# Graph convolution passes: ScalarE makes three of four classes of one-hot rows, and TensorE looks up one more column per block

## The chip, the cores and the metric

One core of a Trainium2 chip runs the whole program. The metric is the device time of one execution in microseconds. The median of three runs of the kernel before is 13509.75 us (13502.95 to 13512.86).

## The reference, cut to what matters

Four graph layers run one after the other on 6250 nodes and 200000 edges that are sorted by destination, each followed by a layer norm. The change touches the third layer alone, which holds three graph convolutions:

```python
def gcn_conv(x, w, b, row, col, ew, n):
    h = x @ w
    deg = jax.ops.segment_sum(ew, col, num_segments=n)
    dinv = jnp.where(deg > 0, jax.lax.rsqrt(deg), 0.0)
    norm = dinv[row] * ew * dinv[col]
    out = jax.ops.segment_sum(norm[:, None] * h[row], col, num_segments=n)
    return out + b
...
x2 = jax.nn.relu(gcn_conv(x, w1, b1, row, col, ew, n))
x3 = jax.nn.relu(gcn_conv(x2, w2, b2, row, col, ew, n))
x4 = jax.nn.relu(gcn_conv(x3, w3, b3, row, col, ew, n))
```

For each edge a row of a node table is looked up by the edge's source, scaled by the edge's weight, and summed over the edges of one destination.

## The kernel before, in words

`graph_pass` does one such convolution. It is called three times: twice with rows of 16 numbers (the narrow passes) and once with rows of 32 (the wide pass). The edges lie as 128 partitions by 1568 columns. A block is 16 columns; a pass has 98 blocks, which alternate between two halves `h` = 0 and 1 with their own buffers. A loop of 49 rounds handles block n = 2i and then n = 2i + 1.

A column's 128 rows are looked up in one of two ways.

- GpSimd gathers them from DRAM by an indirect DMA (L990), one instruction per column. In a narrow pass that is 7 columns for half 0 and 8 for half 1; in the wide pass 10.
- TensorE looks up the others: `ON_CHIP` gives 9 and 8 columns in a narrow pass and 6 and 6 in the wide one. The node table lies on the chip in four classes of 13 nodes per lane. For each class a 0/1 matrix `one_lo` says which lane an edge's source has; a column takes 4 classes times 2 parts of the table, so 8 matmuls (L1030). `multiply(h, 0)` does the first four columns (three in the wide pass), `multiply(h, 1)` the rest. VectorE then picks one of the 13 nodes per lane (`pick`, a product L1078, and `gather`, a reduction L1081).

`one_lo` is made on VectorE by `one_hots` (L1048): four compares per block, one per class, of the keys with the lane's number. The keys of a block come by a DMA from SyncE's queue (L960) that spreads one row of DRAM to 128 partitions.

The order within a pass is written out by hand, engine by engine, with semaphores between. VectorE in block n: `pick(0)`, the compares for block n+1, the small `one_slots` for n+1, `gather(0)`, `pick(1)`, `gather(1)`, then, after the gathered rows have landed, the scaling (L1106), a carry (L1109) and a scan along the block (L1113). ScalarE in block n: after the gathered rows have landed it copies the index of block n+2 (L996), after the scan it copies the result into `run_rows` (L1018), and then it stages four small tiles for block n+2. SyncE in block n: it waits until the compares have read the keys of block n, loads the keys of block n+2 (L960), waits for the `copied` semaphore of block n (which `run_rows` raises), and stores `run_rows` (L975). TensorE is about a block ahead of VectorE: its first multiply of block n+1 waits for the step ONE_HOTS of VectorE's block n, its second for SECOND_MADE, which is `pick(1)`. The semaphore `looked` counts the multiplies that are done.

Of the kernel before, what the change touches and what calls it, by code (L numbers as in the profile page):

```python
# [22 lines left out]
ACT = mybir.ActivationFunctionType  # L23
AX = mybir.AxisListType

P = 128
# [8 lines left out]
IT = T // (2 * B)  # L35
# [10 lines left out]
SENT = 1 + C + LABELS  # L46
RUN = C + LABELS + 2 * C
GROUP_SLOTS = 7
ON_CHIP = {16: (9, 8), 32: (6, 6)}
FIRST_GROUP = {16: 4, 32: 3}  # L50
CLASSES = 4
CLASS = -(-J // CLASSES)
KEY_BLOCKS = -(-T // P)
WIDE_CLASSES = 7
# [851 lines left out]
def graph_pass(nc, sig, table, width, edge, parts, running, final, zeros):  # L906
# [6 lines left out]
    GATHERED = [B - K for K in KS]  # L913
    GROUPS = [[slice(0, FIRST), slice(FIRST, K)] for K in KS]
    MOST = [FIRST, max(KS) - FIRST]
    FIRST_MADE, ONE_HOTS, SECOND_MADE, SCALED, per = 1, 1 + CLASSES, CLASSES + 4, CLASSES + 6, CLASSES + 8
    INIT = 2 * per
    SLOT = 256 if CLASS * width <= 256 else 512
    with ExitStack() as ctx:
# [8 lines left out]
        def sem(name):  # L928
            return ctx.enter_context(nc.semaphore(f"{name}{uid}"))
# [21 lines left out]
            weight = [t[:] for t in pair("weight", [P, B])]  # L951
        gathered, stored, indexed, staged, loaded = ([sem(f"{n}{h}_") for h in range(2)] for n in ("gathered", "stored", "indexed", "staged", "loaded"))
        stepped, looked, copied = (sem(n) for n in ("stepped", "looked", "copied"))
        block = ctx.enter_context(nc.Block())
        running_v = running[0:EP, :].rearrange("(p t) c -> p t c", p=P)

        @block.sync
        def _(sp):
            def load(h, n):
                sp.dma_start(keys[h][:], edge["keys"][bass.ds(n * B, KS[h]), :].rearrange("k e -> (k e)").unsqueeze(0).broadcast_to([P, KS[h] * P])).then_inc(loaded[h], 16)  # L960

            for h in range(2):
                cut = slice(h * width // 2, (h + 1) * width // 2)
                sp.dma_start(running[EP:EP + 1, cut], zeros[0:1, cut]).then_inc(stored[h], 16)
            for h in range(2):
                load(h, h)
            with sp.Fori(0, IT) as i:
                for h in range(2):
                    n = 2 * i + h

                    sp.wait_ge(stepped, INIT + per * (n - 1) + ONE_HOTS)
                    load(h, n + 2)

                    sp.wait_ge(copied, n + 3)
                    sp.dma_start(running_v[:, bass.ds(n * B, B), :], run_rows[h][:]).then_inc(stored[h], 16)  # L975
            for h in range(2):
                sp.wait_ge(stored[h], 16 * (IT + 1))
                sp.wait_ge(loaded[h], 16 * (IT + 1))
# [14 lines left out]
        @block.scalar  # L993
        def _(act):
            def stage_index(h, at):
                nc.scalar.copy(index[h][:], edge["src"][:, bass.ds(at + KS[h], GATHERED[h])]).then_inc(indexed[h], 1)  # L996

            def stage(h, at):
                nc.scalar.activation(slot[h][:], edge["src_slot"][:, bass.ds(at, KS[h])], ACT.Copy)
                nc.scalar.activation(weight[h], edge["weight"][:, bass.ds(at, B)], ACT.Copy)  # L1000
                nc.scalar.activation(keep[h][:], edge["keep"][:, bass.ds(at, B)], ACT.Copy)
                nc.scalar.activation(carried[h][:, :, 1:B], repeat(edge["keep"][:, bass.ds(at + 1, B - 1)], width), ACT.Copy).then_inc(staged[h], 1)

            act.sem_inc(copied, 2)
            stage_index(0, 0)
            stage_index(1, B)
            stage(0, 0)
            stage(1, B)
            with act.Fori(0, IT) as i:
                for h in range(2):  # L1010
                    n = 2 * i + h

                    act.wait_ge(gathered[h], 16 * GATHERED[h] * (i + 1))
                    stage_index(h, (n + 2) * B)

                    act.wait_ge(stepped, INIT + per * (n + 1))
                    act.wait_ge(stored[h], 16 * (i + 1))
                    nc.scalar.activation(run_rows[h][:], run[h][:].rearrange("p c b -> p b c"), ACT.Copy).then_inc(copied, 1)  # L1018
                    stage(h, (n + 2) * B)

        @block.tensor
        def _(pe):
            def multiply(h, g):
                for k in range(KS[h] - FIRST if g else FIRST):
                    at = k * SLOT
                    to = p_slots[g][:, at // 512, at % 512:at % 512 + width * CLASS]
                    e = (g * FIRST + k) * P
                    for q in range(CLASSES):
                        for part_no, part in enumerate(parts):
                            ins = nc.tensor.matmul(to, one_lo[h][:, q, e:e + P], flat(part[:, q, :, :]),  # L1030
                                                   start=q == 0 and part_no == 0, stop=q == CLASSES - 1 and part_no == len(parts) - 1)
                ins.then_inc(looked, 1)

            with pe.Fori(0, IT) as i:
                for h in range(2):
                    n = 2 * i + h

                    pe.wait_ge(stepped, INIT + per * (n - 1) + ONE_HOTS)
                    multiply(h, 0)

                    pe.wait_ge(stepped, INIT + per * (n - 1) + SECOND_MADE)
                    multiply(h, 1)

        @block.vector
        def _(dve):
            def one_hots(h, step):
                for q in range(CLASSES):
                    step(nc.vector.tensor_scalar(one_lo[h][:, q, :], keys[h][:], sig["lanes"][:, q:q + 1], None, ALU.is_equal))  # L1048

            def one_slots(h, step):  # L1050
                step(nc.vector.tensor_tensor(one_hi[h][:], repeat(sig["iota"][:, 0:CLASS], KS[h]), spread(slot[h][:], CLASS), ALU.is_equal))
# [7 lines left out]
            dve.wait_ge(loaded[0], 16)  # L1059
            one_hots(0, lambda ins: ins.then_inc(stepped, 1))  # L1060
            dve.wait_ge(staged[0], 1)
            one_slots(0, lambda ins: ins.then_inc(stepped, per - FIRST_MADE - CLASSES))
            with dve.Fori(0, IT) as i:
                for h in range(2):
                    n, done = 2 * i + h, [0]
# [14 lines left out]
                    def gather(g):  # L1080
                        step(nc.vector.tensor_reduce(rows[h][:, GROUPS[h][g], :], picked[g][:, 0:KS[h] - FIRST if g else FIRST, :, :], AX.X, ALU.add))  # L1081

                    dve.wait_ge(looked, 2 * n + 1)

                    after()
                    pick(0)
# [3 lines left out]
                    one_hots(1 - h, step)  # L1090
                    assert done[0] == ONE_HOTS

                    dve.wait_ge(staged[1 - h], i + 1 + h)
                    one_slots(1 - h, step)
                    after(FIRST_MADE)
                    gather(0)

                    dve.wait_ge(looked, 2 * n + 2)
                    pick(1)
                    assert done[0] == SECOND_MADE  # L1100
                    after()
# [13 lines left out]

            dve.wait_ge(stepped, INIT + per * 2 * IT)
            nc.vector.tensor_copy(final[:, 0:width], run[1][:, :, B - 1]).then_inc(stepped, 1)


def spread_to_edges(nc, sig, block, node_rows, begin_row, edge_rows, table, first_key, first_rows, saved=0):  # L1120
# [903 lines left out]
def gnn(nc, out, x, src, dst, u, ew, labels, label_rows, attrs, spline1, root1, bias01, spline2, root2, bias02,  # L2024
# [3 lines left out]
    with ExitStack() as ctx:  # L2028
# [3 lines left out]
        def sb(name, shape, dt=F32, scope=ctx):  # L2032
            return scope.enter_context(nc.sbuf_tensor(name, shape, dt))

        sig = {n: Signal(ctx.enter_context(nc.semaphore(n))) for n in
               ("copied", "turned", "turned_sb", "product", "saved", "fetched", "pe_step", "act_step", "dve_step", "pool_step", "moved", "rounds")}


        groups = [Signal(ctx.enter_context(nc.semaphore(f"fetched_group{g}"))) for g in range(J // GROUP_SLOTS)]
# [28 lines left out]
        for name in ("ident", "ones", "upper", "shift1", "shift2"):  # L2068
            sig[name] = sb(name, [P, P])
        sig["iota"], sig["lanes"] = sb("iota", [P, P]), sb("lanes", [P, WIDE_CLASSES])  # L2070
        sig["ident_b"], sig["not_earlier"] = sb("ident_b", [P, P], BF16), sb("not_earlier", [P, P], BF16)
        chunk_row = sb("chunk_row", [P, 1])
        zeros = sb("zeros", [P, max(B, J - REST) * C])
# [155 lines left out]
        with ExitStack() as tmp:  # L2229
            h = sb("h0", [P, J, C], F32, tmp)  # L2230
            with ExitStack() as made:
                wide_key, in_class = (sb(n, [P, T], F32, made) for n in ("wide_key", "in_class"))
                rest = sb("x_rest", [P, J, C], F32, made)

                def wide_keys(step):

                    step(V.tensor_scalar(in_class[:], src_hi[:, 0:T], -float(WIDE_CLASS // 2), 1.0 / WIDE_CLASS, ALU.add, ALU.mult))
                    step(V.tensor_scalar(in_class[:], in_class[:], ROUND, None, ALU.add))
                    step(V.tensor_scalar(in_class[:], in_class[:], -ROUND, None, ALU.add))
                    step(V.scalar_tensor_tensor(wide_slot[:, 0:T], in_class[:], -float(WIDE_CLASS), src_hi[:, 0:T], ALU.mult, ALU.add))  # L2240
                    step(V.scalar_tensor_tensor(wide_key[:], in_class[:], float(P), src_lo[:, 0:T], ALU.mult, ALU.add))

                with nc.Block() as block:
                    on_vector(nc, sig, wide_keys, block)
                    turn_keys(nc, sig, block, made, wide_key, wide_key_rows)
                    on_vector(nc, sig, lambda step: split_wide(nc, xs[:], rest, x_parts, step), block)
                    carry_masks(nc, sig, first_dst_f[:], last_dst_f[:], link, step_pen, use_pen, block, made)
# [400 lines left out]
```

## Time and profile before

| what | value |
|---|---|
| median of the runs | 13509.75 us |
| span of the profiled execution | 13509.6 us |
| VectorE busy | 11066.4 us (82%) |
| TensorE matmuls busy | 9536.4 us (71%) |
| GpSimd busy | 9266.9 us (69%) |
| ScalarE busy | 4374.5 us (32%) |
| first keys of the first narrow pass and of the wide pass are issued at | 8250.1 and 10388.5 us |

The shares are over all four layers; the three passes lie between 8250 us and 11660 us of the span. What bounds a pass is read from the rows of that pass, not from the shares. GpSimd's instruction of a gather prepares the DMA's descriptors; between two of them lie 0.30 us that the profile calls issue.

### The profile page before, as it was taken

How to read it: one execution, taken by the hardware profiler on the slowest of the kernel's cores; microseconds unless marked ns; L12 is line 12 of the kernel's file. 1: busy time of each engine (PE TensorE's matmuls, PEld its weight loads, DVE VectorE, ACT ScalarE, POOL GpSimd, SP SyncE). 2: the span in 40 equal slices, each digit the busy share in tenths (PEclk: the TensorE clock that was granted, in tenths of full speed). 3: DMA queues.
4: the chain of work that ended last, by engine and by line, in shares of the span. 5: the costliest groups of instructions: out<-in, count | busy, mean ns of one | idle time of the engine just before them, and what ended most of it. 6: DMA issues, size and time to landing. Idle time of an engine off the chain costs nothing. (4 is left out here: it accounts for less than half of the span.)

```text
span 13509.6 us, 209667 instructions
## 1 busy us (share of the span) xinstructions
PE 9536.4 (71%) x57073; PEld 8046.3 (60%) x57073; DVE 11066.4 (82%) x24500; ACT 4374.5 (32%) x14847; POOL 9266.9 (69%) x9348
## 2 busy tenths in 40 slices
PE   5666667777757766777774546886886888678886
PEld 4555556666645555555552116886886777567775
DVE  8888878888768888888888997886886888589997
ACT  3444434444423333333333331111111111123332
POOL 6777757777667777777774005777776777677776
PEclk8888879999878888888886667998997999699997
DMA  3333324444323333333335761221221222133332
GB/s 89 89 89 85 88 71 125 124 119 124 113 65 100 99 101 101 101 100 97 99 101 195 272 246 41 48 47 39 47 48 38 50 49 49 30 78 87 85 87 68
DMA packets 637171, 1243.59 MB, mean 92 GB/s; under 512 B 206033, under 2 KB 390390, under 8 KB 586530
## 3 DMA queue, kind: packets, MB, share of 16 engines
q1 hardware_dynamic: 322624, 912.21, 19.9%
q0 software_dynamic: 300160, 269.02, 11.8%
q10 hardware_dynamic: 14337, 61.82, 1.2%
q8 instruction: 16, 0.26, 0.0%
q14 instruction: 34, 0.28, 0.0%
HBM read 475.84 MB, written 768.08 MB: 92 GB/s over the span
## 5 line engine op out<-in xcount | busy, mean ns | idle before, releaser
L1030 PE MATMUL p_slots<-part,one_lo 128*128 128x208 f32 (+1 forms) x18032 | 2666.9, 312 | 616.3 <-DVE one_lo L1048 615.9
L990 POOL DMA_INDIRECT rows<-gcn_table,index x2450 | 2442.6, 997 | 883.0 <-issue 727.7
L1030 PEld LDWEIGHTS p_slots<-part,one_lo 128*128 128x128 f32 x18032 | 2584.2, 205 | 699.2 <-DVE one_lo L1048 682.7
L1351 PE MATMUL a_p_slots<-att_part,a_one_lo 128*128 128x456 f32 x8232 | 2007.5, 408 | 585.2 <-DVE y L1414 502.8
L1351 PEld LDWEIGHTS a_p_slots<-att_part,a_one_lo 128*128 128x128 f32 x8232 | 1741.4, 214 | 953.6 <-DVE y L1414 680.7
L1282 POOL DMA_INDIRECT sent<-a_out_rows,a_place x1568 | 1585.5, 1011 | 494.0 <-issue 476.2
L622 PE MATMUL p_slots<-x_part,key_lo 128*128 128x448 f32 x6916 | 1649.2, 393 | 109.7 <-DVE scratch L751 73.3
L556 POOL DMA_INDIRECT msg<-x_rows,index x1372 | 1312.0, 956 | 507.4 <-issue 448.4
L556 POOL DMA_INDIRECT msg<-h_rows,index x1274 | 1234.4, 969 | 490.9 <-issue 383.8
L622 PEld LDWEIGHTS p_slots<-x_part,key_lo 128*128 128x128 f32 x6916 | 1378.1, 206 | 226.3 <-DVE scratch L751 90.3
L788 DVE SCALAR_TENSOR_TENSOR run<-run,keep,msg 128x129 f32<-128x129 f32 (+1 forms) x3136 | 1112.8, 355 | 388.7 <-ACT msg L591 284.2
L1744 POOL DMA_INDIRECT e_rows<-soft_table,e_index x1176 | 1167.4, 993 | 375.6 <-issue 330.8
L1787 PE MATMUL e_p_slots<-soft_part,e_one_lo 128*128 128x456 f32 x5488 | 1243.9, 387 | 125.2 <-DVE e_one_lo L1810 125.2
L1787 PEld LDWEIGHTS e_p_slots<-soft_part,e_one_lo 128*128 128x128 f32 x5488 | 1073.9, 198 | 260.3 <-DVE e_one_lo L1810 146.4
L1273 POOL DMA_INDIRECT a_rows<-att_table,a_index x980 | 998.9, 1019 | 305.7 <-issue 298.4
L1048 DVE TENSOR_SCALAR one_lo<-keys,lanes 128x1152 fp32r<-128x1152 f16 (+2 forms) x1188 | 826.4, 756 | 10.6 <-DMA keys<-key_rows 10.6
L996 ACT COPY index<-src_i 128x8 int32 (+4 forms) x300 | 59.2, 198 | 2286.4 <-DMA rows<-gcn_table,index 2176.6
L591 ACT ACTIVATE msg<-msg,weight 128x64 f32<-128x64 f32 x3136 | 769.1, 340 | 0.5 <-DVE msg L769 0.5
L584 ACT ACTIVATE earlier<-p_same 128x1280 bf16<-128x1280 f32 x392 | 485.2, 1238 | 787.8 <-PE p_same L637 787.8
L1078 DVE TENSOR_TENSOR picked<-p_slots,one_hi 128x832 f32<-128x832 f32 (+1 forms) x588 | 704.1, 1198 | 37.3 <-PE p_slots L1030 27.2
L1081 DVE TENSOR_REDUCE rows<-picked 128x64 f32<-128x832 f32 (+1 forms) x588 | 702.3, 1194 | 10.1
L1367 PE MATMUL a_p_label<-w_labels,a_label 128*128 128x512 f32 x392 | 340.8, 1021 | 467.4 <-DMA a_label_row<-in_label_rows 467.4
(478 smaller groups left out, 17203.7 us busy)
## 6 DMA issues: line engine op xcount, KB each, us to landing
running_dst<-a_run SPq DMA_DIRECT2D x98, 1600.0 KB
running_src<-s_run SPq DMA_DIRECT2D x98, 1600.0 KB
running<-run SPq DMA_DIRECT2D x98, 1032.0 KB
running<-run SPq DMA_DIRECT2D x98, 1024.0 KB
running<-y SPq DMA_DIRECT2D x98, 656.0 KB
s_rows<-sent ACTq DMA_DIRECT2D x98, 584.0 KB, 7.0
begun_x<-zeros SPq DMA_DIRECT2D x98, 512.0 KB
a_xdst<-begun_x SPq DMA_DIRECT2D x98, 512.0 KB
```

The source lines that it names most:

```text
L556: pool.indirect_dma_start(out=msg[h][:, K + k, 0:C], out_offset=None, in_=table, in_offset=offsets(index[h][:, k:k + 1])).then_inc(gathere ...
L591: nc.scalar.activation(msg[h][:, k, C:2 * C], msg[h][:, k, 0:C], ACT.Copy, scale=weight[h][:, k:k + 1]).then_inc(weighed, 1)
L622: ins = nc.tensor.matmul(p_slots[:, bank, 0:C * WIDE_CLASS], key_lo[h][:, c, e:e + P], flat(part[:, c, :, :]), start=c == 0 and part_no == ...
L788: step(nc.vector.scalar_tensor_tensor(run[h][:, k, :], before, keep[h][:, k:k + 1], msg[h][:, k, :], ALU.mult, ALU.add))
L990: pool.indirect_dma_start(out=rows[h][:, KS[h] + k, :], out_offset=None, in_=table, in_offset=offsets(index[h][:, k:k + 1])).then_inc(gath ...
L1030: ins = nc.tensor.matmul(to, one_lo[h][:, q, e:e + P], flat(part[:, q, :, :]), start=q == 0 and part_no == 0, stop=q == CLASSES - 1 and pa ...
L1048: step(nc.vector.tensor_scalar(one_lo[h][:, q, :], keys[h][:], sig["lanes"][:, q:q + 1], None, ALU.is_equal))
L1273: pool.indirect_dma_start(out=rows[h][:, K + k, :], out_offset=None, in_=table, in_offset=offsets(index[h][:, k:k + 1])).then_inc(gathered ...
L1282: pool.indirect_dma_start(out=sent, out_offset=offsets(place[h][:, k:k + 1]), in_=out_rows[h][:, k, :], in_offset=None).then_inc(scattered ...
L1351: ins = nc.tensor.matmul(to[:, k, 0:WIDE_COLUMNS], one_lo[h][:, q, e:e + P], part[:, q, :], start=q == 0 and part_no == 0, stop=q == WIDE_ ...
L1744: pool.indirect_dma_start(out=rows[h][:, KS[h] + k, :], out_offset=None, in_=table, in_offset=offsets(index[h][:, k:k + 1])).then_inc(gath ...
L1787: ins = nc.tensor.matmul(p_slots[g][:, k, 0:WIDE_COLUMNS], one_lo[h][:, q, e:e + P], part[:, q, :], start=q == 0 and part_no == 0, stop=q ...
```

## The change

Four things change in `graph_pass`; outside it one small constant is added (`lane_bias` = -2 times the lanes' numbers).

1. TensorE looks up one column more per block: 10 and 9 in a narrow pass, 7 and 7 in the wide one. GpSimd gathers one less: 6 and 7, and 9.
2. VectorE makes one of the four classes (`OWN` = 1). ScalarE makes the other three in `light`: three Squares of 2 key - 2 lane, which give 0 on a hit and at least 4 elsewhere, and one Relu of 1 minus that over all three classes in place, which gives 1 and 0. `light` for block n+2 stands at the head of ScalarE's block n, ahead of the index copy, and waits for the keys of block n+2 and for both multiplies of block n, whose `one_lo` it overwrites.
3. TensorE's first multiply of a block waits for `lit`, which ScalarE raises after the Relu. SyncE waits for `lit` of block n before it loads the keys of block n+2.
4. VectorE's `gather(0)` stands ahead of `one_slots`.

```diff
-ON_CHIP = {16: (9, 8), 32: (6, 6)}
+ON_CHIP = {16: (10, 9), 32: (7, 7)}
...
+LIT = 3
...
                     sp.wait_ge(stepped, INIT + per * (n - 1) + ONE_HOTS)
+                    sp.sem_inc(sig["rounds"].sem, 1)
+                    sp.wait_ge(lit.sem, lit.base + n + 1)
                     load(h, n + 2)
 
                     sp.wait_ge(copied, n + 3)
...
+            def light(h, n, loads):
+
+                act.wait_ge(loaded[h], 16 * loads)
+                for q in range(OWN, CLASSES):
+                    ins = nc.scalar.activation(one_lo[h][:, q, :], keys[h][:], ACT.Square, bias=sig["lane_bias"][:, q:q + 1], scale=2.0)
+                ins.then_inc(squared.sem, 1)
+                act.wait_ge(squared.sem, squared.base + n + 1)
+                nc.scalar.activation(one_lo[h][:, OWN:CLASSES, :], one_lo[h][:, OWN:CLASSES, :], ACT.Relu, bias=sig["ones"][:, 0:1], scale=-1.0).then_inc(lit.sem, 1)
...
             with act.Fori(0, IT) as i:
                 for h in range(2):
                     n = 2 * i + h
+
+                    act.wait_ge(looked, 2 * n + 4)
+                    light(h, n + 2, i + 2)
 
                     act.wait_ge(gathered[h], 16 * GATHERED[h] * (i + 1))
                     stage_index(h, (n + 2) * B)
...
                     pe.wait_ge(stepped, INIT + per * (n - 1) + ONE_HOTS)
+                    pe.wait_ge(lit.sem, lit.base + n + 1)
                     multiply(h, 0)
...
             def one_hots(h, step):
-                for q in range(CLASSES):
+                for q in range(OWN):
...
+                    after(FIRST_MADE)
+                    gather(0)
+
                     dve.wait_ge(staged[1 - h], i + 1 + h)
                     one_slots(1 - h, step)
-                    after(FIRST_MADE)
-                    gather(0)
...
```

SyncE's queue in the loop of the first narrow pass, before (an ISA or REGISTER_ALU row is one of the sequencer's own; the names in brackets are the semaphores it waits for):

```order
L960 ISA [waits stepped6771]
L960 DMA keys_6771<-key_rows 128x1152
L974 REGISTER_ALU
L975 ISA [waits copied6771]
L975 DMA running<-run_rows_6771 128x256
L971 ISA
L960 ISA [waits stepped6771]
L960 DMA keys_6771<-key_rows 128x1024
```

and of the change:

```order
L976 REGISTER_ALU [waits stepped6773]
L963 ISA [waits lit]
L963 DMA keys_6773<-key_rows 128x1280
L979 REGISTER_ALU
L980 ISA [waits copied6773]
L980 DMA running<-run_rows_6773 128x256
L974 ISA
L963 ISA [waits stepped6773,lit]
L963 DMA keys_6773<-key_rows 128x1152
```

The order on this queue is as it was: load of keys, wait for the copied result, store, load of the next keys. A wait for `lit` is added ahead of each load.

ScalarE's queue in the same loop, half 0, before:

```order
L996 ISA [waits gathered0_6771]
L996 COPY index_6771<-src_i 128x7
L1016 ISA
L1017 REGISTER_ALU [waits stepped6771]
L1018 ACTIVATE run_rows_6771<-run_6771 128x256 [waits stored0_6771]
L999 ISA
L999 ACTIVATE slot_6771<-src_hi 128x9
```

and of the change:

```order
L1011 ISA [waits looked6773]
L1013 ACTIVATE one_lo_6773<-keys_6773,lane_bias 128x1280 [waits loaded0_6773]
L1013 ACTIVATE one_lo_6773<-keys_6773,lane_bias 128x1280 x2
L1015 REGISTER_ALU
L1016 ACTIVATE one_lo_6773<-one_lo_6773,ones 128x3840 [waits squared]
L1032 ISA
L1001 ISA [waits gathered0_6773]
L1001 COPY index_6773<-src_i 128x6
L1035 ISA
L1036 REGISTER_ALU [waits stepped6773]
L1037 ACTIVATE run_rows_6773<-run_6773 128x256 [waits stored0_6773]
```

The three Squares and the Relu now stand between one block's staging and its index copy and `run_rows`, behind two waits: for TensorE and for the keys.

## Rows read from the trace of the kernel before

**Rows 1.** Stretches of the first narrow and the wide pass; columns named in the first line
```profile
core 0: us, PE busy (x) PEld busy (x) DVE busy (x) ACT busy (x) POOL busy (x), PEclk, DMA share, GB/s
8270.00:9210.00 940.00, 806.08 (x6498) 790.07 (x6496) 806.71 (x1144) 139.84 (x575) 721.74 (x709) 0.93 0.23 48
...
10410.00:11630.00 1220.00, 992.62 (x4631) 943.09 (x4629) 1017.71 (x1162) 204.60 (x581) 926.62 (x963) 0.91 0.23 49
```

**Rows 2.** The scan L1113, once per block: count, ns min/median/max, first and last start
```profile
L1113 DVE TENSOR_TENSOR_SCAN run<-carried,p_msg x90: 686/686/689, 8271.0 to 9148.9; 128x256 f32<-128x256 f32 x90
...
L1113 DVE TENSOR_TENSOR_SCAN run<-carried,p_msg x98: 1220/1220/1222, 10410.1 to 11634.8; 128x512 f32<-128x512 f32 x98
```

**Rows 3.** Groups of the first narrow pass, then of the wide: busy us, mean ns | idle before
```profile
L990 POOL DMA_INDIRECT rows<-gcn_table,index x709 | 722.4, 1019 | 218.4 <-issue 215.5 <-DVE p_msg L1109 1.8 <-DVE p_msg L1106 0.9
L1078 DVE TENSOR_TENSOR picked<-p_slots,one_hi 128x832 f32<-128x832 f32 x144 | 146.9, 1020 | 5.6 <-PE p_slots L1030 2.3
...
L1048 DVE TENSOR_SCALAR one_lo<-keys,lanes 128x1152 fp32r<-128x1152 f16 x192 | 144.7, 815 | 0.0
...
L990 POOL DMA_INDIRECT rows<-gcn_table,index x963 | 928.0, 964 | 293.7 <-issue 276.6 <-DVE p_msg L1109 17.1
```

**Rows 4.** Timeline of two narrow blocks: start us, us, engine line op [idle before]
```profile
8603.02 0.67 ACT L1018 ACTIVATE run_rows<-run 128x256 f32<-128x256 f32 x1 [1.40 <-DVE run L1113]
...
8603.80 3.04 DVE L1048 TENSOR_SCALAR one_lo<-keys,lanes 128x1152 fp32r<-128x1152 f16 x4
...
8604.51 0.34 SPq L960 DMA_DIRECT2D keys<-key_rows  x1
8605.11 1.12 POOL L990 DMA_INDIRECT rows<-gcn_table,index  x1 [0.30 <-issue]
...
8606.90 8.29 PE L1030 MATMUL p_slots<-part,one_lo 128*128 128x208 f32 x72 [1.70 <-DVE one_lo L1048]
...
8607.97 0.94 POOL L990 DMA_INDIRECT rows<-gcn_table,index  x1 [0.30 <-issue]
...
8613.11 0.66 ACT L1018 ACTIVATE run_rows<-run 128x256 f32<-128x256 f32 x1 [1.25 <-DVE run L1113]
...
8614.87 0.34 SPq L960 DMA_DIRECT2D keys<-key_rows  x1
```

**Rows 5.** Timeline of two wide blocks
```profile
10709.51 1.08 ACT L1018 ACTIVATE run_rows<-run 128x512 f32<-128x512 f32 x1 [2.17 <-DVE run L1113]
...
10711.42 0.34 SPq L960 DMA_DIRECT2D keys<-key_rows  x1
...
10713.48 11.54 PE L1030 MATMUL p_slots<-part,one_lo 128*128 128x416 f32 x48 [3.93 <-DVE one_lo L1048]
...
10721.80 1.12 ACT L1018 ACTIVATE run_rows<-run 128x512 f32<-128x512 f32 x1 [2.08 <-DVE run L1113]
...
10724.01 0.34 SPq L960 DMA_DIRECT2D keys<-key_rows  x1
...
10725.72 9.35 PE L1030 MATMUL p_slots<-part,one_lo 128*128 128x416 f32 x48 [0.70 <-DVE one_lo L1048]
```

**Rows 6.** First load of keys of a narrow pass and the compare that waits for it
```profile
8250.11 7.04 SPq L960 DMA_DIRECT2D keys<-key_rows  x3
...
8253.61 3.01 DVE L1048 TENSOR_SCALAR one_lo<-keys,lanes 128x1152 fp32r<-128x1152 f16 x4 [3.63 <-DMA keys<-key_rows]
```

**Rows 7.** The keys' DMAs of the wide pass, from issue to landing
```profile
DMA to landing us min/median/max: 3.1/3.4/4.0
```

**Rows 8.** ScalarE by shape over the whole program: busy us, mean ns | idle before
```profile
L1312 ACT ACTIVATE a_out_rows<-a_xdst,a_att 128x64 f32<-128x64 f32 x1568 | 385.1, 334 | 3.2
...
L1776 ACT ACTIVATE y<-e_run 128x1296 f32<-128x1296 f32 x98 | 247.0, 2521 | 370.5 <-DVE e_run L1905 370.5
...
L1002 ACT ACTIVATE carried<-keep 128x240 f32 x196 | 76.7, 391 | 0.0
...
L1002 ACT ACTIVATE carried<-keep 128x480 f32 x98 | 58.1, 592 | 0.0
```

More of the change, by code:

```diff
@@ L915, in graph_pass @@
     MOST = [FIRST, max(KS) - FIRST]
-    FIRST_MADE, ONE_HOTS, SECOND_MADE, SCALED, per = 1, 1 + CLASSES, CLASSES + 4, CLASSES + 6, CLASSES + 8
+    OWN = CLASSES - LIT
+    FIRST_MADE, ONE_HOTS, SECOND_MADE, SCALED, per = 1, 1 + OWN, OWN + 4, OWN + 6, OWN + 8
     INIT = 2 * per
@@ L953, in graph_pass @@
         stepped, looked, copied = (sem(n) for n in ("stepped", "looked", "copied"))
+        squared, lit = sig["squared"], sig["lit"]
         block = ctx.enter_context(nc.Block())
@@ L1008, in _ @@
             stage(1, B)
+            light(0, 0, 1)
+            light(1, 1, 1)
             with act.Fori(0, IT) as i:
@@ L1032, in multiply @@
                 ins.then_inc(looked, 1)
+            pe.sem_inc(looked, 2)
             with pe.Fori(0, IT) as i:
@@ L1061, in _ @@
             dve.wait_ge(staged[0], 1)
-            one_slots(0, lambda ins: ins.then_inc(stepped, per - FIRST_MADE - CLASSES))
+            one_slots(0, lambda ins: ins.then_inc(stepped, per - FIRST_MADE - OWN))
             with dve.Fori(0, IT) as i:
@@ L1081, in gather @@
                         step(nc.vector.tensor_reduce(rows[h][:, GROUPS[h][g], :], picked[g][:, 0:KS[h] - FIRST if g else FIRST, :, :], AX.X, ALU.add))
-                    dve.wait_ge(looked, 2 * n + 1)
+                    dve.wait_ge(looked, 2 * n + 3)
                     after()
@@ L1091, in _ @@
                     assert done[0] == ONE_HOTS
+                    after(FIRST_MADE)
+                    gather(0)
                     dve.wait_ge(staged[1 - h], i + 1 + h)
                     one_slots(1 - h, step)
-                    after(FIRST_MADE)
-                    gather(0)
-                    dve.wait_ge(looked, 2 * n + 2)
+                    dve.wait_ge(looked, 2 * n + 4)
                     pick(1)
@@ L1117, in _ @@
             nc.vector.tensor_copy(final[:, 0:width], run[1][:, :, B - 1]).then_inc(stepped, 1)
+        squared.base += 2 * IT + 2
+        lit.base += 2 * IT + 2
 def spread_to_edges(nc, sig, block, node_rows, begin_row, edge_rows, table, first_key, first_rows, saved=0):
@@ L2035, in gnn @@
         sig = {n: Signal(ctx.enter_context(nc.semaphore(n))) for n in
-               ("copied", "turned", "turned_sb", "product", "saved", "fetched", "pe_step", "act_step", "dve_step", "pool_step", "moved", "rounds")}
+               ("copied", "turned", "turned_sb", "product", "saved", "fetched", "pe_step", "act_step", "dve_step", "pool_step", "moved", "rounds", "squared", "lit")}
         groups = [Signal(ctx.enter_context(nc.semaphore(f"fetched_group{g}"))) for g in range(J // GROUP_SLOTS)]
@@ L2070, in gnn @@
         sig["iota"], sig["lanes"] = sb("iota", [P, P]), sb("lanes", [P, WIDE_CLASSES])
+        sig["lane_bias"] = sb("lane_bias", [P, WIDE_CLASSES])
         sig["ident_b"], sig["not_earlier"] = sb("ident_b", [P, P], BF16), sb("not_earlier", [P, P], BF16)
@@ L2235, in wide_keys @@
                 def wide_keys(step):
+                    step(V.tensor_scalar(sig["lane_bias"][:], sig["lanes"][:], -2.0, None, ALU.mult))
                     step(V.tensor_scalar(in_class[:], src_hi[:, 0:T], -float(WIDE_CLASS // 2), 1.0 / WIDE_CLASS, ALU.add, ALU.mult))
```

## The prediction

> **What bounds the kernel now.** I read the stretches of the passes first, because the page's shares run over four layers. In the first narrow pass VectorE is busy 807 of 940 us, TensorE 806, GpSimd 722 [rows 1]: three engines near their limit. The scan, one per block, gives the period: 89 intervals from 8271.0 to 9148.9 us are 9.86 us a block, and 97 intervals of the wide pass 12.63 [rows 2]. Then the groups. A narrow gather takes 1.019 us and 218.4 us of idle time lie between 709 of them, 0.31 each; 1.33 times 7.5 gathers is 9.9 us, the whole period [rows 3]. Wide, 0.964 + 0.305 is 1.27, times 10 is 12.7 [rows 3]. So GpSimd's issue of gathers bounds all three passes, and nearly all of its idle time is its own issue, not a wait. ScalarE has room: 139.84 us of 940, or 1.5 us of each of 95.3 blocks [rows 1].
>
> **What the change takes away.** One gather of 7.5 goes in a narrow pass: GpSimd's floor becomes 6.5 x 1.33 = 8.6 us. Wide, 9 x 1.27 = 11.4. VectorE's 807 / 95.3 = 8.5 us lose three compares of up to 0.815 (2.4) and gain one column in a product and a reduction, about 2 x 1.02 / 4 = 0.5 [rows 3]: 6.6 us, no bound any more. TensorE does 72 matmuls in 8.29 us in a narrow block [rows 4], 0.115 each; the mean of 76 takes 8.75. Wide it did 48 in 9.35 [rows 5], so 56 take 10.9. If nothing else held, all passes would gain.
>
> In the timeline a gather beside the compares took 1.12 us, one after them 0.94 [rows 4]; the wide mean is 0.964 [rows 3]. The Trainium skill, SBUF — State Buffer, section "Who interferes with whom", says that a VectorE operation in a two-port mode (a tensor_scalar may be one) locks GpSimd out of a port pair that it needs. By that rule the removed compares would bring a wide gather to some 0.95, and 9 x 1.25 = 11.25 instead of 11.4, 15 us less over the pass. I leave the sum at 11.4.
>
> **What it adds to ScalarE.** No row shows Square or Relu, so I price them by other ACTIVATEs. 240 columns take 391 ns and 480 take 592 [rows 8]: 0.84 ns a column. A 64-column one with a per-partition operand takes 334 [rows 8], so 0.28 us stand beside the columns (0.19 without such an operand); both new operations have one as bias. Square of 1280 columns: 1.35 us; of 1152: 1.25; of 896: 1.03. Relu of 3840: 3.50; 3456: 3.17; 2688: 2.53. Consecutive ones overlap by some 0.1 by my estimate, between none and 0.15, and the Relu waits for the last Square (0.1, estimated). `light` then takes 2 x 1.25 + 1.35 + 0.1 + 3.50 = 7.45 for ten columns and 6.8 for nine, 7.1 on the mean; wide 5.55. The lower bound, without the operand's cost, is 6.7. The upper bound is the row of 1296 columns in 2521 ns [rows 8], 1.73 ns a column, or 13.5 us; that one reads a permuted tile and ours are contiguous, so I take the near row.
>
> With its other 1.5 us ScalarE would be busy 8.6 us a narrow block. That alone would still fit into 9.86.
>
> The Trainium skill, ScalarE: Activation LUTs, section "Rules for kernel authors", advises VectorE rather than ScalarE for such simple functions. The rows agree as to price: three compares cost VectorE about 2.4 us, their replacement 7.1. By the rule alone the move loses only if ScalarE ends on the path.
>
> **Why it does end on the path.** The keys decide. SyncE's queue is in order: load keys(n+2), wait for `run_rows`(n), store, load keys(n+3). Before, VectorE wanted keys(n+3) only in its block n+2, more than a block later. Now ScalarE wants keys(n+3) at the head of its block n+1, right behind the staging of block n, while SyncE may load them only after ScalarE's `run_rows`(n). That closes a ring of one block:
>
> - `run_rows`(n) starts to keys(n+3) issued: 8603.02 to 8604.51 and 8613.11 to 8614.87 [rows 4], 1.49 and 1.76, mean 1.63. The added `lit` wait is long fulfilled; for its step I add 0.05 (0 to 0.1).
> - issue to landing: 3.4, from 3.1 to 4.0, for the wide keys of 128 x 768 two-byte numbers [rows 7]; the 128 x 1152 at a narrow pass's start took 8250.11 to 8253.61, so 3.5 [rows 6]. I take 3.5 for 1280 and 1152 columns, and 0.05 to wake.
> - `light`(n+3): 7.1.
> - index copy and start of `run_rows`(n+1), whose scan and gathers are done: 0.05.
>
> The sum is 12.4 us a narrow block, against 9.86. While the keys come, ScalarE stages for about a microsecond and then idles; that wait is new. Behind it on ScalarE stand the Squares, the index copy that GpSimd waits for two blocks ahead, and `run_rows`; TensorE's first multiply waits for the Relu. No other chain needs as much: TensorE 8.75, GpSimd 8.6, VectorE 6.6.
>
> The wide ring: 1.91 and 2.21 [rows 5], mean 2.06, + 0.05 + 3.4 + 0.05 + 5.55 + 0.05 = 11.15. That lies just below GpSimd's 11.4 and above TensorE's 10.9. With three chains so close I take 11.5, between 11.25 and, with no gain, 12.6.
>
> Start of a pass: before, the first narrow scan came 21 us after the first keys' issue [rows 2, 6]. Now `light`(0) stands ahead of the first multiply, and `light`(2) waits for both multiplies of block 0: 7.45 + 7.45 in place of four compares (3.0) and some cover, so about 10 us more per pass, 30 in all (15 to 40). The extra constant and the moved `gather(0)` cost nothing: VectorE has 5 us to spare per block.
>
> The sum: 2 x 98 x (12.4 - 9.86) = +498; 98 x (11.5 - 12.63) = -111; +30. The profiled span is 13509.6 and the median 13509.75, so no correction is due: 13,927, said as 13,925 us.
>
> **Rivals.**
>
> - *The key load is hidden* (faster). If keys land before ScalarE asks, the narrow passes run at TensorE's 8.75, say 9.0 with hand-overs, and the wide at 11.4: 196 x -0.86 - 98 x 1.23 + 20 = -270, 13,240 us. For it: every engine's own work is under the old period. Against: SyncE's order has the load behind `run_rows` in both programs, and `run_rows` now stands behind `light`. Chance 0.09.
> - *TensorE loses its clock and becomes the bound* (slower still). It would idle 3.6 us of each narrow block. The wide pass before had such a gap: after 3.93 us idle, 48 matmuls took 11.54 instead of 9.35 [rows 5], yet the granted clock was 0.91 of 2.4 GHz over the pass [rows 1]. At 1.2 GHz throughout, 76 matmuls would need 17.5 us; halfway, the narrow block is 14.5 and the time 13,925 + 196 x 2.1 = 14,335. Against: one such dip adds 2 to 3 us, 8.75 + 3 is still under 12.4, and the keys' landing gives slack of several us. Chance 0.05. The Trainium skill, TensorE: Matmul & The Clock Gate, section "What's actually happening", has the half clock as the idle default, released by activity; by that rule alone this rival would be likelier, and the trace's 0.91 bears it out only in part.
> - *ScalarE at the permuted row's rate*: `light` of 13.5 us, wide 10.2, periods 18.8 and 15.8: 13,510 + 1,752 + 311 + 30 = 15,600. Chance 0.03.
>
> The forecast keeps 0.83. With each piece at its low end (1.49, 3.1, 6.7, no steps) the narrow ring is 11.4 to 11.6, at the high end (1.86, 4.0, 7.5, 0.2) 13.5. With the wide from 11.25 to 12.6 that gives 13,700 to 14,250; I take 13,690 to 14,130 for eight in ten, which leaves the fast rival and most of the slow ones out. A difference under 0.2% (27 us) can't be told from none: slower 0.88, same 0.03, faster 0.09.
>
> **What would show it.** In the changed trace: narrow scans 12 to 13 us apart; before each first Square an idle stretch of 3 to 4 us that ends with the DMA of the keys; a Relu of 3840 columns near 3.5 us; keys issued 1.5 to 1.9 us after each `run_rows` starts; TensorE waiting for `one_lo` of ScalarE; GpSimd waiting for the index. The prediction is wrong if the Squares start without a wait for keys, if they end up waiting for TensorE, or if the narrow period is under 10 us.

## Result and profile after

The changed kernel takes 13904.47 us (median of four runs, 13892.0 to 13932.39) against 13506.35 for the kernel before: the ratio is 1.0294, 95% interval 1.0281 to 1.0307. It is slower by 398 us, as forecast (13,925). On the chip of a later series it took 13892.41 us and the ratio was 1.0280 (1.0263 to 1.0297).

The profiled execution spans 13901.5 us, 391.9 more than before. Two stretches, in the first narrow pass and in the wide one, with the columns of [rows 1]:

```profile
8400.00:9400.00 1000.00, 810.99 (x6239) 799.22 (x6239) 574.05 (x740) 680.84 (x822) 526.33 (x535) 0.88 0.18 41
11000.00:12000.00 1000.00, 953.75 (x4933) 915.68 (x4932) 841.34 (x794) 651.51 (x884) 759.23 (x791) 1.00 0.24 57
```

In the narrow pass VectorE fell from 86% to 57% and GpSimd from 77% to 53%; TensorE, at 81% after 86%, hardly changed, and ScalarE rose from 15% to 68%. No engine is busy throughout. An engine that is busy 68% of the time and still sets the end is part of a ring with waits in it. The scans of the three passes, as in [rows 2]:

```profile
L1135 DVE TENSOR_TENSOR_SCAN run<-carried,p_msg x98: 686/686/690, 8315.9 to 9493.7; 128x256 f32<-128x256 f32 x98
...
L1135 DVE TENSOR_TENSOR_SCAN run<-carried,p_msg x98: 686/686/690, 9612.3 to 10807.1; 128x256 f32<-128x256 f32 x98
...
L1135 DVE TENSOR_TENSOR_SCAN run<-carried,p_msg x98: 1220/1220/1222, 10929.9 to 12028.4; 128x512 f32<-128x512 f32 x98
```

Over 97 intervals that is 12.14, 12.32 and 11.32 us a block, where it was 9.87, 9.87 and 12.63. The waits of the narrow stretch (engine line, awaited: us in total, times, longest):

```profile
DVE one_hi L1072 <- ACT carried L1007: 374.5, 82, 5.4
POOL rows L995 <- ACT index L1001: 332.8, 82, 4.7
ACT one_lo L1013 <- DMA keys<-key_rows: 316.5, 82, 4.2
PEld p_slots L1049 <- ACT one_lo L1016: 200.6, 66, 4.7
```

VectorE, GpSimd and TensorE all wait for ScalarE, and ScalarE waits once in each of 82 blocks for the keys, 3.9 us each. One turn of the ring, in the timeline:

```profile
8601.24 0.64 ACT L1037 ACTIVATE run_rows<-run 128x256 f32<-128x256 f32 x1
...
8603.12 0.34 SPq L963 DMA_DIRECT2D keys<-key_rows  x1
...
8606.54 3.87 ACT L1013 ACTIVATE one_lo<-keys,lane_bias 128x1280 fp32r<-128x1280 f16 x3 [4.05 <-DMA keys<-key_rows]
...
8610.44 3.50 ACT L1016 ACTIVATE one_lo<-one_lo,ones 128x3840 fp32r<-128x3840 f32 x1
8613.84 0.18 ACT L1001 COPY index<-src_i 128x6 int32 x1
8613.93 0.64 ACT L1037 ACTIVATE run_rows<-run 128x256 f32<-128x256 f32 x1
8613.99 11.53 PE L1049 MATMUL p_slots<-part,one_lo 128*128 128x208 f32 x80 [4.39 <-ACT one_lo L1016]
...
8614.91 0.94 POOL L995 DMA_INDIRECT rows<-gcn_table,index  x1 [3.87 <-ACT index L1001]
```

`run_rows` to the issue of the keys 1.88 us, issue to the first Square 3.42, Squares and Relu 7.40, and `run_rows` follows at once: 12.7 us for a block of ten columns. TensorE starts 0.05 us after the Relu ends, GpSimd soon after the index copy.

The groups of the same two stretches, as in [rows 3, 8]:

```profile
L995 POOL DMA_INDIRECT rows<-gcn_table,index x535 | 527.3, 986 | 474.0 <-ACT index L1001 332.8 <-issue 141.1
L1013 ACT ACTIVATE one_lo<-keys,lane_bias 128x1280 fp32r<-128x1280 f16 x123 | 158.8, 1355 | 163.1 <-DMA keys<-key_rows 163.1
...
L1016 ACT ACTIVATE one_lo<-one_lo,ones 128x3840 fp32r<-128x3840 f32 x41 | 143.3, 3494 | 1.3
...
L995 POOL DMA_INDIRECT rows<-gcn_table,index x791 | 760.7, 962 | 241.1 <-issue 226.7 <-ACT index L1001 6.1 <-DVE run L1135 5.8
L1013 ACT ACTIVATE one_lo<-keys,lane_bias 128x896 fp32r<-128x896 f16 x264 | 256.2, 1034 | 335.4 <-DMA keys<-key_rows 335.4
L1016 ACT ACTIVATE one_lo<-one_lo,ones 128x2688 fp32r<-128x2688 f32 x88 | 223.9, 2544 | 2.9
```

Narrow, 333 of GpSimd's 474 idle us are waits for the index. Wide, its idle time is its own issue, as before; 9 x (0.962 + 0.305) is 11.4 us, within 1% of the period of 11.32.

### The profile page after: what moved, and what is told of

Its sections match the earlier page's. It is cut to its first block and busy times, and to the rows that moved or that the text cites. A ratio compares the mean times of both kernels' runs of the same rounds, so it can differ in the third digit from the quotient of the medians.

```text
span 13901.5 us, 216105 instructions
## 1 busy us (share of the span) xinstructions
PE 9885.1 (71%) x59425; PEld 8398.8 (60%) x59425; DVE 10674.4 (77%) x23610; ACT 6268.1 (45%) x16047; POOL 8921.5 (64%) x9054
## 3 DMA queue, kind: packets, MB, share of 16 engines
q0 software_dynamic: 290752, 265.79, 10.7%
## 5 line engine op out<-in xcount | busy, mean ns | idle before, releaser
L1049 PE MATMUL p_slots<-part,one_lo 128*128 128x208 f32 (+1 forms) x20384 | 2991.2, 311 | 635.9 <-ACT one_lo L1016 599.2
L1049 PEld LDWEIGHTS p_slots<-part,one_lo 128*128 128x128 f32 x20384 | 2921.7, 206 | 705.6 <-ACT one_lo L1016 640.7
L995 POOL DMA_INDIRECT rows<-gcn_table,index x2156 | 2105.2, 976 | 1553.4 <-ACT index L1001 821.9
L1013 ACT ACTIVATE one_lo<-keys,lane_bias 128x1280 fp32r<-128x1280 f16 (+2 forms) x900 | 1033.7, 1212 | 1159.9 <-DMA keys<-key_rows 1143.1
L1016 ACT ACTIVATE one_lo<-one_lo,ones 128x3840 fp32r<-128x3840 f32 (+2 forms) x300 | 922.1, 3074 | 9.8
L1099 DVE TENSOR_TENSOR picked<-p_slots,one_hi 128x832 f32<-128x832 f32 (+1 forms) x588 | 791.1, 1345 | 134.5 <-PE p_slots L1049 127.6
L1072 DVE TENSOR_TENSOR one_hi<-iota,slot 128x130 f32<-128x130 f32 (+2 forms) x297 | 81.5, 275 | 946.8 <-ACT carried L1007 946.8
L1102 DVE TENSOR_REDUCE rows<-picked 128x64 f32<-128x832 f32 (+1 forms) x588 | 787.2, 1339 | 10.2
```

Source lines behind the costliest of these rows:

```text
L995: pool.indirect_dma_start(out=rows[h][:, KS[h] + k, :], out_offset=None, in_=table, in_offset=offsets(index[h][:, k:k + 1])).then_inc(gath ...
L1013: ins = nc.scalar.activation(one_lo[h][:, q, :], keys[h][:], ACT.Square, bias=sig["lane_bias"][:, q:q + 1], scale=2.0)
L1016: nc.scalar.activation(one_lo[h][:, OWN:CLASSES, :], one_lo[h][:, OWN:CLASSES, :], ACT.Relu, bias=sig["ones"][:, 0:1], scale=-1.0).then_in ...
```

## Experiments

Theory A is the ring of the prediction. Theory B is that ScalarE's work bounds the narrow pass wherever the keys land. Theory C is that TensorE with one more column does.

**Keys ahead.** SyncE loads keys(n+3) before it waits for `run_rows`(n).

```diff
+            sp.wait_ge(stepped, INIT - per + ONE_HOTS)
+            sp.wait_ge(lit.sem, lit.base + 1)
+            load(0, 2)
...
-                    sp.wait_ge(stepped, INIT + per * (n - 1) + ONE_HOTS)
+                    sp.wait_ge(stepped, INIT + per * n + ONE_HOTS)
                     sp.sem_inc(sig["rounds"].sem, 1)
-                    sp.wait_ge(lit.sem, lit.base + n + 1)
-                    load(h, n + 2)
+                    sp.wait_ge(lit.sem, lit.base + n + 2)
+                    load(1 - h, n + 3)
...
```

> The changed kernel with one difference: SyncE loads the keys of block n+3 ahead of its wait for run_rows of block n, no longer behind the store. Theory A (the ring run_rows, load of keys, landing, light, next run_rows sets the narrow period): the 1.7 us to the issue and the 3.5 us to landing leave the ring; ScalarE's own 8.6 us and TensorE's 8.75 us remain, so narrow blocks of about 9.1 us (8.8 to 9.6), wide still 11.3 by GpSimd; time 13,300 us (13,220 to 13,420), faster than both kernels. Theory B (ScalarE's work and its hand-overs bound it, wherever keys land): narrow stays near 12.2, time within 50 us of 13,904. Theory C (TensorE with one more column and a falling clock is the bound): also 12.2 and 13,904.

13156.02 us; 0.9755 of before (0.9739 to 0.9771). B and C fall: by the two ratios some 730 us go without any work taken away. The time is also 144 us below A's own figure, and below its range. The stretches, narrow and wide:

```profile
8400.00:9000.00 600.00, 600.00 (x5376) 600.00 (x5375) 494.84 (x637) 582.50 (x706) 457.95 (x459) 1.00 0.27 59
10300.00:11200.00 900.00, 858.40 (x4440) 824.31 (x4439) 753.48 (x714) 593.83 (x791) 682.94 (x713) 1.00 0.25 56
```

TensorE is busy all of the narrow stretch, at the full granted clock of 2.4 GHz (1.00; it was 0.93 before and 0.88 in the change). 5376 matmuls in 600 us are 0.112 us each, and 76 of them 8.5 us, which is the period: 8.50 and 8.51 us. My 9.1 had added hand-overs to TensorE's time, and 8.75 had taken 0.115 us a matmul; this trace shows no idle time of TensorE and 0.112. In the timeline the keys issued here are those that the second row reads 8.35 us later, with no wait noted:

```profile
8604.72 0.34 SPq L963 DMA_DIRECT2D keys<-key_rows  x1
...
8613.07 3.54 ACT L1017 ACTIVATE one_lo<-keys,lane_bias 128x1152 fp32r<-128x1152 f16 x3
```

The wide period stays at 11.30 although ScalarE's wait is gone there too. GpSimd's gathers and its own issue between them fill 884 of the 900 us, so GpSimd bounds the wide pass and the ring only touched it:

```profile
POOL rows L999 <- issue: 200.8, 659, 0.3
```

**Light only.** The change with the old columns.

```diff
-ON_CHIP = {16: (10, 9), 32: (7, 7)}
+ON_CHIP = {16: (9, 8), 32: (6, 6)}
```

> The changed kernel with the columns of before (9 and 8, wide 6 and 6), so ScalarE still makes three classes, behind the same load. Theory A: light is shorter by a column (6.45 us on the mean instead of 7.1), so narrow 11.55 us a block; wide 12.5, bound by GpSimd's ten gathers; time about 13,840 us (13,760 to 13,900), slower than before although TensorE does what it did. Theory C: back to 9.9 us a block and 13,510.

13867.18 us; 1.0289 (1.0272 to 1.0307). The blocks take 11.50, 11.69 and 12.55 us: A's figures within 0.15. TensorE's work is that of before, so C falls a second time. The waits of its first narrow pass:

```profile
ACT one_lo L1013 <- DMA keys<-key_rows: 304.5, 79, 4.1
```

**Columns only.** The kernel before with the new columns.

```diff
-ON_CHIP = {16: (9, 8), 32: (6, 6)}
+ON_CHIP = {16: (10, 9), 32: (7, 7)}
```

> The kernel before with the columns of the change (10 and 9, wide 7 and 7) and all four classes on VectorE. Theory A (the columns are worth something, the loss is all in ScalarE's ring): VectorE's 8.5 us grow by 0.5 for the column and 0.35 for longer compares to 9.3, GpSimd falls to 8.6: narrow 9.4 us, wide 11.6 by VectorE; time 13,320 us (13,230 to 13,420), faster than before. Theory C (a column more is too much for TensorE): no gain or slower than 13,506.

13302.08 us; 0.9865 (0.9849 to 0.9882). 9.36, 9.37 and 11.58 us a block. The columns are worth 1.35% by themselves. What bounds it now, narrow and wide, is VectorE (588.87 of 600, 886.60 of 900):

```profile
8400.00:9000.00 600.00, 554.02 (x4864) 547.92 (x4864) 588.87 (x770) 86.60 (x384) 426.56 (x417) 1.00 0.26 53
10400.00:11300.00 900.00, 842.23 (x4353) 808.00 (x4352) 886.60 (x934) 155.87 (x466) 686.67 (x701) 1.00 0.24 55
```

**Two classes on ScalarE.**

```diff
-LIT = 3
+LIT = 2
```

> The changed kernel with two classes on ScalarE and two on VectorE. Theory A: light loses one Square and a third of the Relu, 2.2 us on the mean, and the ring with it: narrow 10.0 us (9.8 to 10.3), wide 11.3 by GpSimd; time 13,470 us (13,400 to 13,540). Theory C: no change from 12.2 us a block, 13,904.

13460.74 us; 0.9983 (0.9973 to 0.9992). 10.03, 10.18 and 11.30 us a block. The ring shortened by what `light` lost: 2.1 us measured, 2.2 expected. Its wait for the keys is still there in each of 80 blocks, about as long as in the change, 4.0 us:

```profile
ACT one_lo L1013 <- DMA keys<-key_rows: 316.3, 80, 4.3
```

**Light last.** The landing hidden in another way: `light` behind `run_rows` and staging.

```diff
-                    act.wait_ge(looked, 2 * n + 4)
-                    light(h, n + 2, i + 2)
-
...
                     stage(h, (n + 2) * B)
+
+                    act.wait_ge(looked, 2 * n + 4)
+                    light(h, n + 2, i + 2)
```

> The changed kernel with light for block n+2 moved on ScalarE from the head of block n to its end, behind index copy, run_rows and staging; SyncE as in the change. The landing of the keys is then hidden behind light of the block before, as in the run with keys ahead. Theory A, followed through: the landing leaves the one-block ring, but a ring over two blocks closes: light 7.1, both multiplies 8.5, second pick and reduction, scaling and scan 4.2, run_rows and staging 1.6, together 21.4, so 10.7 us a narrow block; wide 24.5 / 2 = 12.3. Time 13,700 us (13,600 to 13,850): between the change and the run with keys ahead. Rival D (only the hidden landing counts, however it is hidden): 8.5 and 11.3 us, 13,160. Theory B (ScalarE's work alone): 12.2 us, 13,904.

14068.96 us; 1.0417 (1.0399 to 1.0434). Rival D falls: a hidden landing is worth nothing if another ring closes. My figure was wrong too. The periods are 12.19 and 13.25 instead of 10.7 and 12.3. Narrow blocks alternate between 7.6 and some 17 us, and the sum over two is 24.4, not 21.4. Most of the missing 3 us is TensorE's. It idles 5.1 us in each pair and comes back at a lower clock; here are its start after one such gap, the pick that waits for the first 32 matmuls, and the stretches up to that pick and after it (columns as in [rows 1], the granted clock third from the end):

```profile
8711.59 18.63 PE L1049 MATMUL p_slots<-part,one_lo 128*128 128x208 f32 x136 [5.14 <-ACT one_lo L1016]
...
8718.75 1.02 DVE L1099 TENSOR_TENSOR picked<-p_slots,one_hi 128x832 f32<-128x832 f32 x1 [8.28 <-PE p_slots L1049]
```

```profile
8711.60:8718.40 6.80, 6.80 (x32) 6.80 (x33) 0.00 (x0) 6.77 (x10) 4.68 (x5) 0.51 0.28 72
8718.50:8730.00 11.50, 11.50 (x105) 11.50 (x105) 8.69 (x11) 2.47 (x8) 3.75 (x4) 1.00 0.02 3
```

Here 32 matmuls take 6.8 us at 1.2 GHz in place of 3.6 at 2.4. This gap is among the worst: over the 40 gaps between 8400 and 9400 us the first 32 matmuls take 5.3 to 6.9 us, 5.8 on the mean, at a mean granted clock of 0.62. So the clock puts 2.2 of the 3 us on a ring that has TensorE in it. The rest was mis-sized: this ring always closes over the half with ten columns, so its multiplies are 80 matmuls (0.45 us more than the mean half) and its `light` 7.4 us (0.3 more). In the wide pass the first 24 matmuls after a gap take 6.6 us on the mean, where the quickest took 4.6; that is the 2 us that two blocks take beyond my 24.5. In the change itself TensorE idles 4.4 us and is slow after it too (80 matmuls in 11.53 us above, 9.0 at 0.112), but the ring of the keys has slack for that.

**Keys ahead and two classes.** On top of keys ahead:

```diff
-LIT = 3
+LIT = 2
```

> Keys ahead and two classes instead of three on ScalarE. If TensorE alone bounds the narrow passes with keys ahead (76 matmuls of 0.112 us are 8.5), nothing changes: 8.5 and 11.3 us a block, 13,156 us (13,120 to 13,190). If ScalarE, 97% busy there, is a second bound, narrow falls to about 8.3 and the time to 13,110 or less. If VectorE with two classes (7.4 us) gets in the way, it is slower than 13,190.

13152.09 us; 0.9734 (0.9717 to 0.9750). 8.48, 8.48 and 11.40 us a block, the same as with three classes. ScalarE fell to 431 of 600 us and nothing came of it, so ScalarE was no second bound. TensorE, which is never idle, sets the period; but GpSimd, whose gathers and own issue fill 586 of the 600 us, is only 2% behind. By an estimate from these rows a column moved either way would lengthen the block: 84 matmuls take 9.4 us and 7.5 gathers 9.6. ScalarE now waits for TensorE:

```profile
8400.00:9000.00 600.00, 600.00 (x5376) 600.00 (x5375) 547.27 (x708) 431.08 (x638) 454.16 (x458) 1.00 0.24 58
```

```profile
ACT one_lo L1017 <- PE p_slots L1053: 165.4, 70, 3.1
POOL rows L999 <- issue: 131.5, 427, 1.3
```

**Constant only.** The kernel before with the added constant, its one instruction and the two semaphores, all unused: the first pass of the change began 40.1 us late, before any of its new work.

```diff
-               ("copied", "turned", "turned_sb", "product", "saved", "fetched", "pe_step", "act_step", "dve_step", "pool_step", "moved", "rounds")}
+               ("copied", "turned", "turned_sb", "product", "saved", "fetched", "pe_step", "act_step", "dve_step", "pool_step", "moved", "rounds", "squared", "lit")}
...
+        sig["lane_bias"] = sb("lane_bias", [P, WIDE_CLASSES])
...
+                    step(V.tensor_scalar(sig["lane_bias"][:], sig["lanes"][:], -2.0, None, ALU.mult))
```

> The kernel before with only the added constant, its one VectorE instruction and the two added semaphores; nothing uses them. It asks where the 40 us come from that the changed kernel is late at the start of the first pass (8290.2 against 8250.1). If the shift of the tensors' places by the constant causes them: 20 to 40 us slower than before, and passes that begin 20 to 40 us later. If they are a difference of one execution from the next: within 0.1% of before.

13533.94 us; 1.0014 (1.0004 to 1.0024). It begins its first graph pass at 8278.4 us.

**The change again.** No edit; the same kernel on the chip of three other runs.

> The changed kernel itself, on the chip of the other runs. 13,904 us within 0.3%, narrow 12.15 and 12.3, wide 11.33 us a block; the first pass begins at 8290 us if its lateness belongs to the program, or anywhere from 8245 to 8290 if it belongs to the execution.

13892.41 us; 12.17, 12.33 and 11.35 us a block. The first pass begins at 8272.5, so of the 40 us some are the execution's.

**No constant.** Keys ahead with the lanes themselves as bias.

```diff
-                    ins = nc.scalar.activation(one_lo[h][:, q, :], keys[h][:], ACT.Square, bias=sig["lane_bias"][:, q:q + 1], scale=2.0)
+                    ins = nc.scalar.activation(one_lo[h][:, q, :], keys[h][:], ACT.Square, bias=sig["lanes"][:, q:q + 1], scale=-1.0)
...
-        sig["lane_bias"] = sb("lane_bias", [P, WIDE_CLASSES])
...
-                    step(V.tensor_scalar(sig["lane_bias"][:], sig["lanes"][:], -2.0, None, ALU.mult))
```

> Keys ahead, three classes on ScalarE, and no added constant: Square(lane - key) with the lanes that are there as bias and scale -1 gives 0 on a hit and at least 1 elsewhere, so the same Relu of 1 minus it gives the same rows. If the constant's place in the memory is what lengthens the second spline pass (17.3 to 17.6 us a block in the eight traces with it, 17.15 in the two without), that pass returns to 17.15 us, the first graph pass begins at 8240 to 8255 us, and the time is 13,125 us (13,100 to 13,145), the fastest. If the added semaphores do it, 17.4 and 13,155.

13135.26 us; 0.9727 (0.9714 to 0.9740). It beats both kernels and has the lowest ratio of all, but its interval overlaps those of the other two runs with keys ahead (0.9755 and 0.9734, on other chips), so it is not shown to be the fastest. Its first pass begins at 8248.3.

**Semaphores only.** The kernel before with the first line of the constant's diff alone:

```diff
-               ("copied", "turned", "turned_sb", "product", "saved", "fetched", "pe_step", "act_step", "dve_step", "pool_step", "moved", "rounds")}
+               ("copied", "turned", "turned_sb", "product", "saved", "fetched", "pe_step", "act_step", "dve_step", "pool_step", "moved", "rounds", "squared", "lit")}
```

> The kernel before with the two added semaphores alone, which nothing uses. If the constant is the cause: second spline pass 17.15 us a block, first graph pass from 8240 to 8255 us, time as before within 0.1%. If the semaphores are: 17.4 us, some 25 us later, 0.15% slower.

13511.12 us; 1.0000 (0.9991 to 1.0009). The semaphores cost nothing that shows. The lateness lies in the second spline pass, which ends some 4600 us ahead of the changed code: in the profile of the change it begins when it did before, and its last block starts 41 us later. Its blocks in a stretch that begins at 1990 us, by one small ScalarE copy per block (count, first and last start), in the kernel before:

```profile
L562 ACT ACTIVATE weight<-u_s x94: 215/215/216, 1993.7 to 3590.9; 128x16 f32 x94
```

in the change:

```profile
L563 ACT ACTIVATE weight<-u_s x92: 215/215/216, 1994.0 to 3598.3; 128x16 f32 x92
```

with the constant only:

```profile
L562 ACT ACTIVATE weight<-u_s x92: 215/216/217, 1992.4 to 3586.3; 128x16 f32 x92
```

and with keys ahead and no constant:

```profile
L563 ACT ACTIVATE weight<-u_s x94: 215/216/216, 1992.3 to 3590.0; 128x16 f32 x94
```

That is 17.2, 17.6, 17.5 and 17.2 us a block. The kernels with the constant have an unchanged pass that is 1 to 3% slower. The constant brings 28 bytes in each partition, ahead of tensors that are allocated later, and one VectorE instruction that runs once. That the shifted places do it, and not the instruction's place in the code, was not tested on its own, and why either should matter there stays open.

## Why the prediction was right

The terms against the two profiles:

| term | forecast us | measured us |
|---|---|---|
| narrow passes | +498 | +457.5 (220.3 + 237.2) |
| wide pass | -111 | -126.2 |
| starts of the passes | +30 | +14.7 |
| ends of passes and the rest | 0 | +5.8 |
| second spline pass, ahead of the change | 0 | +40.1 |
| sum | +417 | +391.9 |

- *The bound before* holds: with columns only, GpSimd's floor fell and the passes gained at once, until VectorE took over at 9.37.
- *The ring* is right step by step. In the two narrow passes `run_rows` to issue (each pair of rows like those above, averaged) is 1.70 and 1.86 us (forecast 1.68), issue to the first Square 3.41 (3.55), `light` 7.09 (7.1), the rest 0 (0.05). Breaking it at SyncE took 3.7 us off the block; shortening it by a class took 2.1.
- *The price of Square and Relu* came from other ACTIVATEs and met: 1.355 us forecast 1.35, 3.494 forecast 3.50.
- *The narrow term* is 40 us too large: the landing was 0.15 us shorter than the 3.5 that I took from a pass's first load, and the step to wake ScalarE is in it already.
- *The wide term*: the ring is 11.2 us and GpSimd 11.4 by its groups; the measured 11.32 shows that two near-equal chains needed none of the 0.1 us that the forecast of 11.5 added for them.
- *The pass's start* cost half of what I gave it: the first scan comes 25.7 us after the first keys' issue (before 20.9).

```profile
8290.16 11.50 SPq L963 DMA_DIRECT2D keys<-key_rows  x3
...
8301.18 27.92 PE L1049 MATMUL p_slots<-part,one_lo 128*128 128x208 f32 x232 [19.07 <-ACT one_lo L1016]
...
8312.26 3.87 ACT L1013 ACTIVATE one_lo<-keys,lane_bias 128x1280 fp32r<-128x1280 f16 x3 [4.46 <-PE p_slots L1049]
```

  `light`(0) is in the way, as forecast, and `light`(2) waits for TensorE; but the first scan needs neither `light`(2) nor `run_rows`.
- *Missed*: the 40 us of the second spline pass (in the second profile of the change the first pass began 22 us late). I cost the constant at nothing. Without it the forecast would have been 65 us too high, so part of the closeness is luck. The narrow, wide and start terms were together some 70 us too high.
- *The rivals.* "The key load is hidden" is the kernel that the run with keys ahead made: 13,156 where I had worked out 13,240. TensorE at a lower clock did not bind the change (VectorE waited for it 38.9 us in the narrow stretch) but did bind the run with light last. The price of that rival was mis-added: halfway between 8.75 and 17.5 us is 13.1, not 14.5, and the time with it would be about 14,060 us, not 14,335. Its dip of 2 to 3 us was met: the 80 matmuls above took 2.5 us more than at full clock.
- *The range* has two small slips: its low pieces (1.49, 3.1 and 6.7) add up to 11.3, not 11.4 to 11.6, and the longest `run_rows` to issue in [rows 4] is 1.76, not 1.86. Neither would move the range enough to leave the measured time out.
- By the rule of the Trainium skill, SBUF — State Buffer, section "Who interferes with whom", that a VectorE operation in a two-port mode blocks GpSimd, I had estimated a wide gather of 0.95 us with the compares gone. It is 0.962 on the mean, against 0.964 before [rows 3], with one compare a block left; no gain of that kind showed in the wide pass. Narrow it fell from 1.019 to 0.986.

## What to carry to other kernels

When work moves to an idle engine, follow its input back through the queue that brings it: here a load stood behind a store that waits for the very engine that now wants the load, and that order had been harmless as long as the reader was a block later. Count the ring, not the busy time; a ring of 12.2 us held three engines at 53 to 81%. And of the two ways to hide the landing, the one that left the other hand-overs where they were gained, and the one that moved them closed another ring.

## What had not been expected of the hardware

With a constant of 28 bytes per partition and its one instruction a pass of other code was 1 to 3% slower, even where nothing used the constant (eight traces with it lie at 17.3 to 17.6 us a block, four without at 17.15 to 17.25). And TensorE held its full clock, 1.00, through whole stretches: with keys ahead, where it was never idle, and with columns only, where it waited 45 of 600 us, 1.4 at the longest. The narrow pass before, with waits of up to 2.4 us, got 0.93.
